# Two-layer gated cross-attention on one core: data-free semaphore increments in place of GpSimd's one-column multiplications

## The reference, cut to what matters

```
x = x + tanh(g_xattn[0]) * L0_xattn(layernorm(x), ctx)       # "difference" attention, then an exact-GELU MLP
x = x + tanh(g_ffn[0])   * L0_ffn(layernorm(x))              # a linear layer in fp8 values, one scale for all of x
x = x + tanh(g_xattn[1]) * L1_xattn(layernorm(x), ctx, mask) # 16-head softmax attention
x = x + tanh(g_ffn[1])   * L1_ffn(layernorm(x))              # layernorm, a SiLU MLP with 1024 hidden features
```

## Time and profile before

| | |
|---|---|
| median of three runs | 1754.54 us (1752.0 to 1756.51) |
| the profiled execution | 1753.54 us, its span 1751.8 us |
| mean granted TensorE clock | 0.971 of full speed |
| PE busy | 1610.3 us, 92% of the span |
| DVE busy | 1336.3 us, 76% |
| ACT busy | 1055.9 us, 60% |
| POOL busy | 1033.6 us, 59% |

### The profile page before, as it was taken

One profiled execution on the slowest core, in us unless ns is written; L12 is line 12 of the kernel. 1 busy time (PEld: TensorE's weight loads), 2 busy tenths in 40 slices (PEclk: granted clock), 3 DMA queues, 4 the chain that ended last, 5 costly groups with the idle time before them and its releaser, 6 DMA issues.

```text
span 1751.8 us, 42950 instructions
## 1 busy us (share of the span) xinstructions
PE 1610.3 (92%) x14411; PEld 1255.7 (72%) x14411; DVE 1336.3 (76%) x3213; ACT 1055.9 (60%) x1894; POOL 1033.6 (59%) x1873
## 2 busy tenths in 40 slices
PE   5999999999999993577999999999999999999997
PEld 4888888888888882344677777767777776767666
DVE  5677777777777766768888888888888888887643
ACT  6666666666666553255656666665666666565654
POOL 5566676667666645324656575665656566564536
PEclk9999999999999996688999999999999999999999
DMA  7312211221122002342233232322223232222200
GB/s 210 101 61 74 76 60 60 75 75 60 60 79 71 7 1 71 96 123 79 82 83 88 79 93 75 90 85 82 81 83 90 72 90 85 83 84 84 66 15 20
DMA packets 215099, 133.59 MB, mean 76 GB/s; under 512 B 45936, under 2 KB 214256, under 8 KB 214768
## 3 DMA queue, kind: packets, MB, share of 16 engines
q1 hardware_dynamic: 215024, 132.61, 25.9%
HBM read 101.07 MB, written 25.17 MB: 72 GB/s over the span
## 4 chain that ended last, share of the span: by engine, by line
PE 34%; DVE 8%; ACT 6%; issue 5%; POOL 5%; SPq 1%; DVEq 0%; DMA 0%; ACTq 0%; POOLq 0%
PE b_bank L1639 17%; PE b_bank L1718 5%; PE b_scoreT L1696 4%; PE b_scoreT L1700 3%; PE b_score L1679 2%; ACT L31 2%; DVE b_v L1522 2%; DVE b_nm L1459 2%; ACT b_Y L1337 2%; ACT b_E L1277 1%; PE b_bank L1647 1%; POOL b_YT L1204 1%; DVE b_hn L1440 1%; PE b_bank L1733 1%; POOL b_rs L1214 1%
## 5 line engine op out<-in xcount | busy, mean ns | idle before, releaser
L1459 DVE TENSOR_REDUCE b_nm<-b_score 128x4 bf16<-128x1024 f32 x256 | 314.5, 1228 | 115.2 <-PE b_score L1679 107.7
L1277 ACT ACTIVATE b_E<-b_scoreT 128x1024 f32<-128x1024 f32 x256 | 262.0, 1023 | 196.9 <-PE b_scoreT L1700 196.0
L1159 POOL TENSOR_TENSOR b_pool_fence<-b_pool_fence 128x1 f32<-128x1 f32 x288 | 67.6, 235 | 299.3 <-ACT b_Y L1337 258.5
L761 PE MATMUL bank<-W2T,G 128*128 128x256 f32 x1024 | 231.2, 379 | 0.0
L761 PEld LDWEIGHTS bank<-W2T,G 128*128 128x128 f32 x1024 | 192.1, 190 | 24.8
L31 ACT ACT_TABLE_LOAD x156 | 200.1, 1283 | 9.9 <-PEq L876 6.6
L1337 ACT ACTIVATE b_Y<-b_bank,b1f 128x256 f32<-128x256 f32 x256 | 107.3, 470 | 159.1 <-PE b_bank L1639 158.7
L1639 PE MATMUL b_bank<-b_hT,f 128*128 128x256 bf16 x1536 | 188.7, 273 | 11.6 <-ACT b_Y L1337 11.3
L1639 PE MATMUL b_bank<-f,b_YT 128*128 128x256 bf16 x1536 | 183.5, 273 | 2.9 <-POOL b_YT L1204 1.9
L328 POOL TENSOR_TENSOR pool_fence<-pool_fence 128x1 f32<-128x1 f32 x256 | 48.3, 201 | 233.5 <-DVE mv L538 145.9
L728 PE MATMUL bank<-hT,W1T 128*128 128x256 bf16 x1536 | 178.3, 273 | 6.6 <-ACT G L498 2.5
(11 more groups left out here) (211 smaller groups left out, 3538.1 us busy)
## 6 DMA issues: line engine op xcount, KB each, us to landing
b_Q<-q_dram SPq DMA_DIRECT2D x256, 64.0 KB, 2.5
b_K<-k_dram SPq DMA_DIRECT2D x256, 64.0 KB, 2.5
xin<-in_x SPq DMA_DIRECT2D x32, 256.0 KB, 4.3
ctxn<-in_ctx SPq DMA_DIRECT2D x32, 256.0 KB, 2.7
mask_in<-in_mask SPq DMA_DIRECT2D x32, 256.0 KB, 3.0
X<-in_x SPq DMA_DIRECT2D x32, 256.0 KB, 4.2
ctxt<-in_ctxT SPq DMA_DIRECT2D x32, 256.0 KB, 4.4
b_ctxt<-in_ctxT SPq DMA_DIRECT2D x32, 256.0 KB, 2.7
```

Of the source, the lines that this page charges most:

```text
L761: last = nc.tensor.matmul(out_ps[:, t], G[w.parity][:, h, t * P:(t + 1) * P], W2T[:, h], start=h == 0, stop=h == HC - 1)
L1277: nc.scalar.activation(E[:, pair:pair + 2], scoreT_ps[:, :, :, :], ACT.Exp).then_inc(sig["E"], 1)
L1459: nc.vector.tensor_reduce(pair, score_ps[:, :, :, :], AX.X, ALU.max, negate=True).then_inc(sig["nm"], 1)
```

## The change: what it does

In both `fence()` functions the multiplication is replaced by an increment of a semaphore named `fence`. No instruction waits for it. It stands where the multiplication stood and now carries the waits. The constant tile is still set at the start of each phase; all else is unchanged.

```diff
@@ -324,8 +324,7 @@
         def _(pool):
             def fence():
 
-                k = next(pool_columns)
-                nc.gpsimd.tensor_tensor(pool_fence[:, k:k + 1], pool_fence[:, 0:1], pool_fence[:, 0:1], ALU.mult)
+                pool.sem_inc(sig["fence"], 1)
 
```

## The result

The changed kernel takes 1747.83 us in the median of 7 runs (1743.06 to 1750.57), the kernel before 1753.64 us beside it (7 runs, 1752.0 to 1756.51): a ratio of 0.9964, interval 0.995 to 0.9978. Run again in the last experiment, it came to 0.9955 (0.994 to 0.9969). Forecast were 1748.2 us and -0.36%. The same kernel came out 5.8 us faster in one comparison and 7.9 in the other, so it is luck that the forecast hit -0.36% to the digit. Its profiled execution took 1748.64 us (span 1746.9) against 1753.54 (span 1751.8).

A forecast was written before the change was run, and what follows sets the result against it. PE's stream bounds phase A; in phase B a POOL and DVE path bounds 16 iterations. 5.3 + 1.0 = 6.3 us off 1753.54 gives 1747.2, plus 1.0 for a median: 1748.2 us (-0.36%), range 1745.3 to 1756.

The forecast's parts named there:

- What bounds: PE's own stream bounds phase A (98.8% busy); in phase B a POOL and DVE path bounds 16 iterations, 30.65 against 30.27 us.
- four signs named for being right: Phase B chain free of POOL's `b_rh`; PE's line 1481 wait gone; SiLUs 30.3 us apart; POOL's step 0.15 us after release.
- A fence whose wait is over: POOL's sequencer handles the increment while the engine is busy, so the next step follows directly: 0.15 us saved each.
- A waiting fence: On POOL, release to next step falls from 0.23 to 0.15 us where the fence still waits: 0.08 us saved.
- Four fences, 0.53 us on the path: In phase B's bound iterations, three fences from the first SiLU and one before `silu_parts(h, 1)` save 0.53 us; 0.38 needed.
- Rival B: In phase B POOL's `silu_parts` takes the turn from DVE's line 1432, eating gain: 1 to 3 us left, 1752.5; chance 0.20.
- 16 x 0.33 = 5.3 us: All 16 bound phase B iterations fall to PE's pace, gaining 0.33 us each, chosen between 0.20 (PE's wait) and 0.38 (SiLU starts).
- The edges: Six chain fences outside the bound iterations give 0.6 us, phase A's last batch some 0.4: together 1.0 us, ends 0 and 1.5.
- Rival C: In phase B, POOL running ahead takes the turn from one more DVE instruction between lines 1440 and 1481: slower, 1763; chance 0.09.
- Rival D: POOL's sequencer reaches each increment only when the engine is done, costing 0.14 us against 0.15: nothing moves, 1754; chance 0.18.

The follow-up runs named there:

- phaseA_only: Kernel before with increments for multiplications in phase A's fence only, phase B unchanged; 1754.82 us against 1755.04, ratio 0.9997.
- rest_inc: Kernel before with increments at phase B's other six fences per batch; those before the first SiLU part and two inverse deviations stay multiplications; ratio 0.9962.
- phaseB_only: Kernel before with increments for multiplications in phase B's fence only, phase A unchanged; 1746.37 us against 1755.04, ratio 0.9948.
- extra5: Changed kernel with five more multiplications in front of phase B's output bias; ratio 0.9971 to the kernel before.
- double_inc: Kernel before with two increments in place of each phase B fence multiplication, phase A unchanged; ratio 0.9949.
- plus1: Kernel before with one more multiplication in front of phase B's output bias; ratio 0.9964.
- double_mult: Kernel before with two multiplications per fence in phase B instead of one, phase A unchanged; ratio 1.0023.

## Why the prediction was right, point by point

*What bounds.* Right. PE's stream covers phase A (phaseA_only 0.9987 to 1.0006), and the 16 long intervals are where the 24 intervals got shorter. Of the four signs named for being right three came. The fourth, POOL's step 0.15 us behind its release, did not: it is 0.22 us behind the SiLU's end.

*A fence whose wait is over: 0.15 us each.* Measured 0.13 to 0.15: right, and the reason with it. Of the 232 increments 180 take 17 ns; 125 of these run inside an instruction of the engine, 53 in the gap of 0.08 us in front of an instruction that waits for the one before, a gap that was there already.

*A waiting fence: 0.08 us.* Too high. It gave 0.01 us on the path and 0.02 in the phase A case shown; over the 64 steps of phase A that start `inverse_std` for `mv` and `mvo` the median from DVE's end to POOL's step went from 0.24 to 0.20 us. The step that failed: the price after the change was taken from a semaphore instruction of 17 ns that had waited, 0.14 us from release to engine, plus 0.01. An increment with pending waits takes 43 ns, and the engine starts 0.19 us after it began.

*Four fences, 0.53 us on the path.* The count failed: six, 0.71 us. `context_parts` and the output bias were left out, though DVE runs behind POOL's large instructions up to the rounding term. Rival B did count `context_parts`, but wrote 0.8 us for what 0.53 and 0.15 make 0.68. The count had no effect on the sum, since all beyond the needed 0.38 is lost at PE's pace either way.

*16 x 0.33 = 5.3 us.* Right in size: 5.41 by the first SiLUs, or 0.34 each. But the reason given for 0.33, a choice between 0.20 and 0.38, isn't what made it: the prediction knew one length of an unbound interval, and there are two. The need was 0.37 us in ten of the 16, now 30.28, and 0.28 in six, now 30.37. That the choice came so near is luck. That everything beyond is lost is shown by rest_inc and phaseB_only: paths 0.27 us apart, and the same 727.6.

*The edges: 1.0 us.* Not found in the profiles, nor excluded by the times: 5.8 and 7.9 us, each within some 2.5 us, fit 5.4 and 6.4 alike, and phaseB_only's 6.8 to 11.6 lie above 5.4. Outside the 24 intervals the profiled pair has 0.5 us in the other direction: 5.41 of the 24, and a span shorter by 4.9. Of that, phase A began 0.72 us earlier and the stretch behind batch 25 took 1.26 us longer. That last stretch has a spell of 3.4 us at 1.2 GHz from 1721.5 us on, which before it had not at that place; the windows of 1715 to 1730 us (length, PE, PEld, DVE, ACT, POOL, clock, DMA), before and after:

```profile
1715.00:1730.00 15.00, 12.34 (x111) 10.48 (x109) 7.55 (x20) 6.65 (x12) 9.24 (x17) 1.00 0.06 19
```

```profile
1715.00:1730.00 15.00, 12.87 (x102) 10.41 (x101) 7.07 (x16) 6.52 (x11) 9.20 (x14) 0.89 0.06 19
```

Over the profiles of all these kernels the first W2 matmul lies between 52.1 and 56.6 us and the last stretch between 164.3 and 168.9, without order in the edits. The one part of the edge that shows through is phase A's drain: from the start of its last W2 matmul to the end of its last row maximum 9.20 to 9.21 us in every kernel with single multiplications there, 9.04 to 9.08 with single increments. That is 0.15 us, where 0.4 was forecast. The rest of the edge term stays open.

*Rival B* didn't come: line 1430 keeps 0.41 us. But what it is made of, a turn that is won or lost, turned out to be the stronger force. The argument against B, that a DVE instruction that asks first has gone first, doesn't hold: `scaled` in the earlier trace rows started at 1166.76 us, ahead of POOL's line 1173 at 1166.86, and took 2.10 us. extra5 shows the mask's instruction at 0.78 us, blocked as B had it, yet covered by a shorter path ahead of it.

*Rival C* didn't come. `scaled` did lose its turn in every interval, as C feared for one more instruction, at 0.93 us (1.95 for 1.02); by then the path was 0.7 us shorter than the bound kind's, and it ended at 13.31, just as the quick kind of before at 13.39. Of those 0.93 us the rounding term gave 0.51 back (0.83 us for 1.34), and the rest is the 0.42 us by which line 1438 ends earlier. That was nearer than the prediction made it appear.

*Rival D* is refuted for POOL at work and nearly right for POOL idle: there an increment costs what a multiplication did, less 0.01 to 0.04 us.

Where the explanation of the whole has to be mended: the gain wasn't bound to instructions taken away. Shorter fences brought the low part in time, and so did more multiplications at one place, by the order of starts between POOL and DVE.

What stays open: why the kernel before has an interval of the quick kind in between. In both kinds `scaled` starts 0.09 us ahead of POOL's next instruction, within some ns; which of the two then waits isn't to be read from the profile.

No version beats the changed kernel: those with the lowest ratios (phaseB_only, double_inc) overlap its intervals and have the same sum.

## What to carry to other kernels

A small instruction on an engine that shares its turns with another has no price of its own: before taking it out or putting it in, list the long instructions of both engines side by side and ask which start order it changes. Where the path that it shortens is only some tenths of a microsecond longer than the bound engine's pace, the gain is that difference times the iterations in which it exists, however many instructions go. Here an increment cost nothing where the engine was still busy, and about what a one-column multiplication costs where it stood idle.

## What the runs showed of the hardware that I had not expected

- An increment that ends POOL's idle time takes 43 ns on the sequencer, and the engine starts 0.19 us after that one's start; most others take 17 ns, and 15 of 232, waiting while the engine is busy, 629 to 715. A second increment delays an idle engine's next step by 0.08 us.
- DVE's rounding term of 128 x 512 takes 0.44 us beside one-column multiplications of POOL and 0.83 to 1.34 beside its large ones. The one-column ones hardly block it, though they are instructions of the same engine. A blocked one ends 0.28 us behind POOL's large instruction.
- The Trainium skill (SBUF — State Buffer, Who interferes with whom) lets whoever issues first hold the shared pair for its instruction. plus1 agrees: 0.11 us of lead for DVE, and it runs at 0.44 us; 0.03 us of lead for POOL, and it takes 0.98. `scaled` doesn't: it starts 0.09 us ahead of POOL's instruction in both kinds and is quick in one of them only. Nor does line 1441 of double_mult, blocked though it starts 0.12 us ahead. What the profile gives as starts doesn't settle who holds the pair.
- POOL's relief in phase A, 38.3 us, came back as 37.5 us of DVE busy time, with PE's unchanged.
